# First attention: q/k projection half a step earlier with more buffers, blank writes moved to the dense stage, x in pieces, constants reordered

## The chip, the cores and the metric

One core of a Trainium2 chip runs the whole kernel. The metric is the device time of one execution in microseconds (us).

## What is computed

The kernel is four layers, each with a residual sum and a layer norm. The change is in the first, an attention block over 64-token buckets; the dense layers behind it take over one job of it. The first attention, cut:

```python
h = _ln(x, ln1_g, ln1_b)                      # x: 16 x 256 tokens x 128 channels
q, k, v = split(h @ w_qkv + b_qkv, 3)         # 16 heads of 8 channels, buckets of 64
kc = concatenate([kp, kb]); vc = concatenate([vp, vb])   # previous bucket and own
scores = einsum('bnihd,bnjhd->bnhij', qb, kc) * scale    # causal in the own bucket
attn = softmax(where(mask, scores, -inf))
x = x + einsum('bnhij,bnjhd->bnihd', attn, vc) @ w_out + b_out
# then an MLP, a gated dense layer of 8 experts, a second attention and a routed layer
```

## The kernel before

The first attention (`attention_0`) works through 16 batches (`NB`) of 256 tokens, software pipelined. The table `PARTS_0` is the order, written out by hand: four parts a step, each a list of (what, stage, k). `parts_0` runs 21 steps; in step s an entry works on batch s - stage. Every engine walks the same table and executes, in order, what it has under that name, so an engine's queue is its own extract of the table, and semaphores tie the queues together. Under the names stand:

- `stats` (VectorE: mean and variance of x, L445 to L449), `power` (GpSimd: inverse deviation, four small instructions, L319 to L322), `norm` (ScalarE: hn, L371), `lift` (TensorE transposes hn into the left half of the PSUM tile WA, L516, ScalarE copies it to hT; from batch 4 on, the same entry also transposes the attention output of four batches back into the right half, L520, copied to aT).
- `qk` (TensorE: q and k projections into WA, L526 and L527; ScalarE: copy with bias, L385, then the high part in f16, L389; GpSimd: the low part, L338). `spread` (SyncE): high and low part are written to a buffer in memory (`spill`, L282, L284), and six DMAs read them back (L298) into the row layout of the tiles qs (2 buffers) and ks (3 buffers).
- `scores` (TensorE: two units of eight matmuls, L548, and one mask matmul, L554; VectorE: row maxima, L463), four times a step; `mpad` and `shift` (VectorE, TensorE L560, VectorE L480: the maxima are subtracted from q, into q2); `weights` (TensorE: transposed scores in ST, L570; ScalarE: exponential into pt, L395; GpSimd: causal mask, L351; two units each); `values` (TensorE: pt times va into OT, L582); `copy`, `back` (L591), `output` (L601) to the result x1; `sums` (GpSimd: x1 + x, L344).
- `vproj` (TensorE L533, VectorE L457): value projection into va (3 buffers).

S and ST each have two halves, one per unit, so TensorE runs at most two units ahead of the maxima or of the exponentials. The tile MI is shared by `shift` and `back`, WB by `vproj` and `output`.

SyncE issues the DMAs of the loop: the spread of a batch; behind batch 0 the rest of x (tiles 12 to 31) and the gate; behind batch 1 the dense stage's first weights (`fetch_dense`); and from batch 1 on five blank writes a batch (L307, 268 KB each, 72 in all), which fill a table in memory for the last layer.

VectorE and GpSimd set the constants at the start: the k buffers are cleared and get a column added (L420), the v buffers get zeros and a column of ones, and the output bias is split into bf16 rows (`constants_of`). All of it stands in front of step 1.

In the dense stage, SyncE loads one broadcast gate row per job (L796) into a ring of six, paced by the semaphore `g_used`.

Of the kernel before, what the change touches and what calls it, by code (L numbers as in the profile page):

```python
# [9 lines left out]
P = 128  # L10
# [125 lines left out]
def unpacked(m, name):  # L136
# [4 lines left out]
    for part, shape in parts:  # L141
# [11 lines left out]
    [("qk", 1, 0), ("scores", 2, 0), ("shift", 3, 1), ("stats", 0, 0), ("weights", 3, 0), ("values", 4, 3),  # L153
     ("copy", 4, 1), ("spread", 1, 0)],
    [("scores", 2, 1), ("mpad", 2, 0), ("output", 5, 0), ("back", 4, 1), ("power", 0, 0), ("weights", 3, 1),
     ("values", 3, 0)],
    [("scores", 2, 2), ("vproj", 1, 0), ("shift", 2, 0), ("norm", 0, 0), ("weights", 3, 2), ("sums", 5, 0),
     ("values", 3, 1), ("copy", 3, 0)],
    [("lift", 0, 0), ("scores", 2, 3), ("mpad", 2, 1), ("back", 3, 0), ("weights", 3, 3), ("values", 3, 2)]]
STAGES_0 = 6  # L160


def parts_0(step):

    for s in range(NB + STAGES_0 - 1):
        for part in PARTS_0:
            for what, stage, k in part:
                if what == "lift":
                    if s < NB + 4:
                        step(what, s, k)  # L170
                elif 0 <= s - stage < NB:
                    step(what, s - stage, k)


def attention_0(nc, d, keep, rows, spill, stages):
# [3 lines left out]
    with ExitStack() as ctx:  # L179
# [10 lines left out]
        blank = m.sb("blank", [P, 4, ROW])  # L190
        blanks = rows.rearrange("(i p r) c -> p i r c", p=P, r=4)
        blank_set, blanked = m.sem("blank_set"), m.sem("blanked")
# [12 lines left out]
        qs = [m.sb(f"qs{p}", [P, 4, TB], F16) for p in range(2)]  # L205
        ks = [m.sb(f"ks{p}", [P, 4, BK + TB], F16) for p in range(3)]
        va = [m.sb(f"va{p}", [P, 4, H, 32]) for p in range(3)]
# [27 lines left out]
        lift_full, lift_free = m.sem("lift_full"), m.sem("lift_free")  # L235
        qk_full, qk_own, low_done = m.sem("qk_full"), m.sem("qk_own"), m.sem("low_done")
# [18 lines left out]
        LOADS, CLEARS, PRESET = 3, 5, 3  # L255
        READS = 16 * len(SPREAD)
        first_in, half_set, warm = m.sem("first_in"), m.sem("half_set"), m.sem("warm")
        preset, bias_own, bias_set = m.sem("preset"), m.sem("bias_own"), m.sem("bias_set")
        scrap = m.sb("scrap", [P, 2])

        def rows_landed(eng, n):
            eng.wait_ge(x_first if n < 2 else x_mid if n < 6 else x_rest, 16)
# [6 lines left out]
        def _(sp):  # L269
# [8 lines left out]
            def step(what, n, k):  # L278
                if what == "spread":
# [5 lines left out]
                    if n == 0:  # L285
                        sp.wait_ge(preset, PRESET)

                    wait(sp, mt_free, n * 2 - 2)
                    wait(sp, st_full, n * 8 - 16)
                    sp.wait_ge(spilled_high, 16 * (n + 1))  # L290
                    for part in range(2):
                        if part == 1:
                            sp.wait_ge(spilled_low, 16 * (n + 1))
                        for w, r, of in SPREAD:
                            if of == part:
                                dst = ks[n % 3][r::4, :, BK:BK + TB] if w else qs[n % 2][r::4, :, :]
                                src = spill[n % 2, of, w].rearrange("(a i) t -> i a t", a=4)
                                sp.dma_start(dst, src).then_inc(spread_done[n % 2], 16)  # L298
                    if n == 0:
                        sp.dma_start(x[:, 12:NT, :], d["x"][:, 12:NT, :]).then_inc(x_rest, 16)  # L300
                        sp.dma_start(keep["gate0"][:], d["gate0"]).then_inc(gate_in, 16)
                    if n == 1:
                        keep["fetch_dense"](sp)
                        sp.wait_ge(blank_set, 1)
                    if n:
                        for i in range(5 * n - 5, min(5 * n, BLANKS * NC_)):
                            sp.dma_start(blanks[:, i], blank[:]).then_inc(blanked, 16)  # L307

            parts_0(step)
            sp.wait_ge(blanked, 16 * BLANKS * NC_)  # L310

        @block.gpsimd
        def _(pool):
# [15 lines left out]
            pool.memset(va[2][:], 0.0).then_inc(zeroed, 1)  # L329
            pool.wait_ge(zeroed, 3)  # L330
            pool.memset(va[2][:, :, :, HD:HD + 1], 1.0).then_inc(cleared, 1)
            pool.memset(blank[:], BLANK).then_inc(blank_set, 1)

            def step(what, n, k):
                if what == "qk":
# [22 lines left out]
        def _(act):  # L358
# [6 lines left out]
            def step(what, n, k):  # L365
# [8 lines left out]
                if what == "lift":  # L374
                    act.wait_ge(lift_full, n + 1)
                    if n < NB:
                        ins = act.activation(hT[:, BK:BK + TB], WA[:, 0:TB], ACT.Identity, scale=g1, bias=s1)
                    if n >= 4:
                        ins = act.activation(aT[:], WA[:, TB:2 * TB], ACT.Copy)
                    ins.then_inc(lift_free, 1)  # L380
# [24 lines left out]
        def _(dve):  # L405
# [4 lines left out]
            for v in ks:  # L410
                dve.memset(v[:], 0.0).then_inc(bias_own, 1)

            def constants_of():
                dve.wait_ge(zeroed, 2)
                for v in va[0:2]:
                    dve.memset(v[:, :, :, HD:HD + 1], 1.0).then_inc(cleared, 1)
                dve.wait_ge(first_in, 32)
                dve.wait_ge(bias_own, 3)
                for i, v in enumerate(ks):
                    ins = dve.tensor_scalar(v[:].rearrange("p a t -> p (a t)"), v[:].rearrange("p a t -> p (a t)"),  # L420
                                            cols[:, 5:6], None, ALU.add)
                ins.then_inc(preset, 1)
# [3 lines left out]
                dve.wait_ge(bias_own, 4)  # L426
                t = Tally(dve, bias_own, 0, 0)
                t.n = 4
# [9 lines left out]
            def step(what, n, k):  # L438
                if what == "stats":
# [10 lines left out]
                    if n == 0:  # L450
                        constants_of()
                if what == "vproj":
                    dve.wait_ge(vproj_full, n + 1)
                    if n == 0:
                        dve.wait_ge(zeroed, 3)
                    wait(dve, pv_done, n * 8 - 16)
                    dve.tensor_tensor(va[n % 3][:, :, :, 0:HD],  # L457
# [18 lines left out]
                if what == "shift":  # L476
# [3 lines left out]
                    dve.tensor_tensor(q2[:, k], qs[n % 2][:, :, k * P:(k + 1) * P], MT,  # L480
# [20 lines left out]
        def _(pe):  # L501
# [7 lines left out]
            def step(what, n, k):  # L509
                if what == "lift":  # L510
                    wait(pe, lift_free, n)
                    wait(pe, high_done, min(n, NB))
                    if n < NB:
                        pe.wait_ge(hn_done, n + 1)
                        for a in range(2):
                            ins = pe.transpose(WA[:, a * P:(a + 1) * P], hn[:, a, :], ident[:])  # L516
                    if n >= 4:
                        pe.wait_ge(back_free, n * 2 - 6)
                        for a in range(2):
                            ins = pe.transpose(WA[:, TB + a * P:TB + (a + 1) * P], ob[n % 2][:, a, :], ident[:])  # L520
                    ins.then_inc(lift_full, 1)
                if what == "qk":
                    pe.wait_ge(lift_free, n + 1)
                    if n == 0:
# [4 lines left out]
                if what == "vproj":  # L529
                    wait(pe, x1_done, n - 3)  # L530
# [5 lines left out]
                if what == "scores":  # L536
# [5 lines left out]
                    for u in (2 * k, 2 * k + 1):  # L542
                        wait(pe, s_free, n * 8 + u - 1)
                        r = slice(32 * (u % 4), 32 * (u % 4) + 32)
                        for v in range(2):
                            w = 2 * (u // 4) + v
                            for a in range(4):
                                pe.matmul(S[BK * v:BK * v + BK, u % 2, a * P:(a + 1) * P],  # L548
                                          qs[n % 2][r, a, w * BK:(w + 1) * BK],
                                          ks[n % 3][r, a, w * BK:w * BK + P],  # L550
# [11 lines left out]
                if what == "weights":  # L562
                    t = k // 2
                    pe.wait_ge(mt_free, n * 2 + t + 1)
                    for u in (2 * k, 2 * k + 1):
                        wait(pe, exp_done, n * 8 + u - 1)
                        r = slice(32 * (u % 4), 32 * (u % 4) + 32)
                        for v in range(2):
                            for a in range(4):
                                ins = pe.matmul(ST[:, u % 2, (4 * v + a) * BK:(4 * v + a + 1) * BK],  # L570
                                                ks[n % 3][r, a, (2 * t + v) * BK:(2 * t + v) * BK + P],
                                                q2[r, t, a, v * BK:(v + 1) * BK], start=True, stop=True)
                        ins.then_inc(st_full, 1)
                if what == "values":
                    t = k // 2
                    wait(pe, ot_free, n * 2 + t)
                    pe.wait_ge(va_done, n + 1)
                    for u in (2 * k, 2 * k + 1):
                        pe.wait_ge(causal_done, n * 8 + u + 1)
                        for v in range(2):  # L580
                            for a in range(4):
                                ins = pe.matmul(OT[32 * a:32 * a + 32, (u % 4) * P + v * BK:(u % 4) * P + (v + 1) * BK],  # L582
                                                va[n % 3][:, 2 * t + v, 4 * a + u % 4, :],
# [1829 lines left out]
```

## Time and profile before

| | us |
|---|---|
| median of three runs (1057.59 to 1060.05) | 1059.03 |
| the profiled execution | 1057.45 |
| its span, first to last instruction | 1055.7 |
| busy TensorE / VectorE / ScalarE / GpSimd | 920.4 / 822.1 / 743.7 / 429.4 |
| mean granted TensorE clock, 1 being 2.4 GHz | 0.944 |

Busy is the time in which an engine executes instructions; the rest is idle, and the trace names what ended it. The first attention ends on TensorE at 238.7 us; the dense layers follow to about 680 us. In the timeline, a row is a group of like instructions in a row: start, length in us, engine, line, operation, output and inputs, count, and in brackets the idle time before and what ended it. SPq is SyncE's queue; its rows are the issuing of DMAs.

### The profile page before, as it was taken

What the parts mean: (1) busy time and instruction counts of PE and PEld (TensorE: products, weight loads), DVE (VectorE), ACT (ScalarE), POOL (GpSimd) and SP (SyncE); (2) the same over time, 40 slices, a digit from 0 to 9 for tenths busy, and PEclk for the clock granted to TensorE, in tenths of its full rate; (3) what the DMA queues carried; (4) which work ended last, traced back from release to release, by engine and by line L of the source; (5) the groups of instructions that cost most, each with busy time, mean ns of one, the idle gap of its engine ahead of it and who ended that gap; (6) DMA issues with size and microseconds to landing.
All of it is one profiled execution on the core that took longest, in us unless ns stands there. A gap on an engine that the chain in (4) does not pass through costs nothing. (4 is left out here: it accounts for less than half of the span.)

```text
span 1055.7 us, 28520 instructions
## 1 busy us (share of the span) xinstructions
PE 920.4 (87%) x9982; PEld 586.6 (56%) x9982; DVE 822.1 (78%) x2266; ACT 743.7 (70%) x1460; POOL 429.4 (41%) x600
## 2 busy tenths in 40 slices
PE   4899999984888999999999999678888875899995
PEld 2677777762444444444444444246556643788862
DVE  5567777746888999868899999858888866888854
ACT  2466666645889988888888878347677643688854
POOL 4356666653355000000000000023578877667653
PEclk8689999997999999999999999979999985999998
DMA  4545554500001200032222222011011102232218
GB/s 143 180 137 178 169 166 160 166 28 21 1 21 60 72 1 1 5 101 74 77 70 78 83 67 74 20 54 31 24 51 53 55 27 74 76 85 84 84 49 219
DMA packets 81946, 82.34 MB, mean 78 GB/s; under 512 B 9466, under 2 KB 58876, under 8 KB 81808
## 3 DMA queue, kind: packets, MB, share of 16 engines
q1 hardware_dynamic: 72608, 69.33, 21.5%
q0 software_dynamic: 4544, 8.60, 2.5%
q10 hardware_dynamic: 4656, 2.59, 1.0%
q8 instruction: 84, 1.38, 0.5%
q14 instruction: 54, 0.44, 0.1%
HBM read 45.71 MB, written 35.68 MB: 77 GB/s over the span
## 5 line engine op out<-in xcount | busy, mean ns | idle before, releaser
L840 ACT ACTIVATE d__hf<-d__HB,dense__d 128x512 f32<-128x512 f32 x288 | 184.7, 679 | 39.1 <-PE d__HB L1079 38.1
L899 DVE TENSOR_TENSOR d__hl<-d__hf,d__hh 128x1024 f16<-128x1024 f32 x144 | 173.5, 1219 | 19.9 <-ACT d__hh L845 17.8
L813 POOL TENSOR_SCALAR d__rstd<-d__mv 128x4 f32<-128x4 f32 x16 | 13.9, 868 | 353.1 <-DVE d__mv L1022 353.1
L845 ACT ACTIVATE d__hh<-d__hf 128x1024 f16<-128x1024 f32 x144 | 152.2, 1057 | 4.6
L463 DVE TENSOR_REDUCE a__mx<-a__S 128x4 f32<-128x512 f32 x128 | 82.1, 684 | 64.1 <-PE a__S L554 64.0
L395 ACT ACTIVATE a__pt<-a__ST 128x512 f32<-128x512 f32 x128 | 69.4, 594 | 63.7 <-PE a__ST L570 63.5
L1077 PE MATMUL d__YB<-d__hh,d__w2h 128*128 128x512 f16 x288 | 109.7, 381 | 2.5 <-DVE d__tmp L956 2.5
L1077 PE MATMUL d__HB<-d__xh,d__w1h 128*128 128x512 f16 x288 | 110.6, 384 | 0.0
L1078 PE MATMUL d__HB<-d__xl,d__w1h 128*128 128x512 f16 x288 | 110.5, 384 | 0.0
L1079 PE MATMUL d__HB<-d__xh,d__w1l 128*128 128x512 f16 x288 | 110.3, 383 | 0.0
L1078 PE MATMUL d__YB<-d__hl,d__w2h 128*128 128x512 f16 x288 | 109.7, 381 | 0.0
L1079 PE MATMUL d__YB<-d__hh,d__w2l 128*128 128x512 f16 x288 | 109.4, 380 | 0.0
L351 POOL TENSOR_SCALAR_AFFINE_SELECT a__pt<-a__pt 128x512 f32<-128x512 f32 x128 | 81.3, 659 | 56.5 <-ACT a__pt L395 56.3
L1338 POOL DMA_INDIRECT parts<-c__ys,c__dest x78 | 81.0, 1038 | 39.1 <-issue 16.8
L1824 POOL DMA_INDIRECT rows<-b__xr,b__slot x64 | 63.8, 996 | 21.5 <-issue 17.0
L1356 ACT ACTIVATE c__hf<-b__SS,c__bias 128x256 f32<-128x256 f32 x156 | 61.0, 474 | 7.3 <-PE b__SS L1565 6.2
L1492 DVE TENSOR_TENSOR c__hl<-c__hf,c__hh 128x512 f16<-128x512 f32 x78 | 54.3, 696 | 2.7
L1077 PEld LDWEIGHTS d__YB<-d__hh,d__w2h 128*128 128x128 f16 x288 | 28.3, 98 | 35.9 <-DVE d__tmp L956 3.9
L1079 PEld LDWEIGHTS d__HB<-d__xh,d__w1l 128*128 128x128 f16 x288 | 28.4, 99 | 35.0 <-issue 1.7
L1077 PEld LDWEIGHTS d__HB<-d__xh,d__w1h 128*128 128x128 f16 x288 | 30.4, 106 | 31.1 <-issue 1.4
L1079 PEld LDWEIGHTS d__YB<-d__hh,d__w2l 128*128 128x128 f16 x288 | 28.3, 98 | 34.3 <-issue 0.6
L582 PE MATMUL a__OT<-a__pt,a__va 128*32 128x64 f32 x2048 | 44.8, 229 | 1.6 <-POOL a__pt L351 0.9
(405 smaller groups left out, 2418.8 us busy)
## 6 DMA issues: line engine op xcount, KB each, us to landing
rows<-a__blank SPq DMA_DIRECT2D x72, 268.0 KB, 3.4
d__G<-gates SPq DMA_DIRECT2D x64, 256.0 KB, 3.2
c__xin<-rows SPq DMA_DIRECT2D x39, 134.0 KB, 2.3
dense__stage<-e_w SPq DMA_DIRECT2D x16, 256.0 KB, 2.9
b__stage<-e_w SPq DMA_DIRECT2D x32, 128.0 KB, 2.2
a__qs<-spill SPq DMA_DIRECT2D x48, 64.0 KB, 2.3
a__ks<-spill SPq DMA_DIRECT2D x48, 64.0 KB, 2.5
spill<-a__high SPq DMA_DIRECT2D x16, 128.0 KB, 4.0
```

Of the source, the lines that this page charges most:

```text
L351: pool.affine_select(out=v, in_=v, compare_op=ALU.is_ge, fill=0.0, base=BK, pattern=[[0, 8], [1, BK]], channel_multiplier=-1).then_inc(cau ...
L395: act.activation(pt[:, u % 4, :], ST[:, u % 2, :], ACT.Exp, scale=scale).then_inc(exp_done, 1)
L463: dve.tensor_reduce(mx[:, u // 4, :, u % 4], S[:, u % 2, :].rearrange("p (a j) -> p a j", a=4), AX.X, ALU.max).then_inc(s_free, 1)
L840: act.activation(hf[:, q, f], HB[:, f], gelu, scale=1.0 / WS, bias=b1[:, at:at + 1]).then_inc(s_["h_free"], 1)
L845: act.activation(hh[:, j % (LEAD + 1), f - 1:f + 1], hf[:, q, f - 1:f + 1], ACT.Copy).then_inc(s_["hi_done"], 1)
L899: dve.tensor_tensor(hl[:, p, f], hf[:, q, f], hh[:, p, f], ALU.subtract).then_inc(s_["lo%d_done" % i], 1)
L1077: pe.matmul(dst, wh, vh, start=begin, stop=False)
L1078: pe.matmul(dst, wh, vl, start=False, stop=False)
L1079: return pe.matmul(dst, wl, vh, start=False, stop=end)
L1338: pool.indirect_dma_start(parts, bass.IndirectOffsetOnAxis(dest[b % RING][:, a:a + 1], 0), ys[b % RING][:, a, :], None, bounds_check=2 * T ...
L1356: ins = act.activation(hf[b % 2][:, f], HB[:, b % 2, f // 2, f % 2], ACT.Gelu, scale=1.0 / WS, bias=bias[:, f, b:b + 1])
L1824: pool.indirect_dma_start(rows, bass.IndirectOffsetOnAxis(slot[n % SENT][:, k, a:a + 1], 0), words[n % SENT][:, a, :], None, bounds_check= ...
```

## The change

- `PARTS_0` has seven stages (22 steps). `norm` and `lift` of a batch come in the step after its `stats`, `qk` in part 2 of that step, `scores` at stage 3. GpSimd's part of `qk` is an entry of its own, `low`; the output's transpose is one too, `turn`, at stage 5.
- q tiles have 3 buffers, k and v tiles 4. The waits for old readers match.
- The 72 blank writes are issued in the dense stage, one behind each gate load, a second one behind each of the first eight. The tile and its semaphore move to `keep`, and a memset on GpSimd fills it, as before.
- Tiles 12 to 31 of x come in five pieces, behind the spreads of batches 0 to 4. The gate comes behind batch 2, the dense weights behind batch 6.
- The k buffers are set by one copy each, behind the statistics of batches 0 to 3, the bias rows behind those of batch 4; GpSimd sets the ones of all v buffers.

```diff
@@ -150,14 +150,14 @@
...
-    [("qk", 1, 0), ("scores", 2, 0), ("shift", 3, 1), ("stats", 0, 0), ("weights", 3, 0), ("values", 4, 3),
-     ("copy", 4, 1), ("spread", 1, 0)],
-    [("scores", 2, 1), ("mpad", 2, 0), ("output", 5, 0), ("back", 4, 1), ("power", 0, 0), ("weights", 3, 1),
-     ("values", 3, 0)],
-    [("scores", 2, 2), ("vproj", 1, 0), ("shift", 2, 0), ("norm", 0, 0), ("weights", 3, 2), ("sums", 5, 0),
-     ("values", 3, 1), ("copy", 3, 0)],
-    [("lift", 0, 0), ("scores", 2, 3), ("mpad", 2, 1), ("back", 3, 0), ("weights", 3, 3), ("values", 3, 2)]]
-STAGES_0 = 6
+    [("norm", 1, 0), ("scores", 3, 0), ("shift", 4, 1), ("weights", 4, 0), ("values", 5, 3), ("copy", 5, 1)],
+    [("scores", 3, 1), ("mpad", 3, 0), ("lift", 1, 0), ("output", 6, 0), ("back", 5, 1), ("weights", 4, 1),
+     ("values", 4, 0)],
+    [("qk", 1, 0), ("scores", 3, 2), ("shift", 3, 0), ("stats", 0, 0), ("weights", 4, 2), ("low", 1, 0),
+     ("spread", 1, 0), ("sums", 6, 0), ("values", 4, 1), ("copy", 4, 0)],
+    [("scores", 3, 3), ("mpad", 3, 1), ("vproj", 1, 0), ("power", 0, 0), ("back", 4, 0), ("weights", 4, 3),
+     ("values", 4, 2), ("turn", 5, 0)]]
+STAGES_0 = 7
...
 def parts_0(step):
@@ -165,10 +165,7 @@
...
-                if what == "lift":
-                    if s < NB + 4:
-                        step(what, s, k)
-                elif 0 <= s - stage < NB:
+                if 0 <= s - stage < NB:
@@ -202,9 +196,9 @@
...
-        qs = [m.sb(f"qs{p}", [P, 4, TB], F16) for p in range(2)]
-        ks = [m.sb(f"ks{p}", [P, 4, BK + TB], F16) for p in range(3)]
-        va = [m.sb(f"va{p}", [P, 4, H, 32]) for p in range(3)]
+        qs = [m.sb(f"qs{p}", [P, 4, TB], F16) for p in range(3)]
+        ks = [m.sb(f"ks{p}", [P, 4, BK + TB], F16) for p in range(4)]
+        va = [m.sb(f"va{p}", [P, 4, H, 32]) for p in range(4)]
@@ -252,14 +247,18 @@
...
-        LOADS, CLEARS, PRESET = 3, 5, 3
+        LOADS, CLEARS, PRESET = 3, 2, 3
...
+        ones_set = m.sem("ones_set")
...
         def rows_landed(eng, n):
-            eng.wait_ge(x_first if n < 2 else x_mid if n < 6 else x_rest, 16)
+            if n < 6:
+                eng.wait_ge(x_first if n < 2 else x_mid, 16)
+            else:
+                eng.wait_ge(x_rest, 16 * ((n - 6) // 2 + 1))
@@ -282,32 +281,29 @@
...
-                    if n == 0:
-                        sp.wait_ge(preset, PRESET)
-                    wait(sp, mt_free, n * 2 - 2)
-                    wait(sp, st_full, n * 8 - 16)
+                    if n < 4:
+                        sp.wait_ge(preset, PRESET + n + 1)
+                    wait(sp, mt_free, n * 2 - 4)
+                    wait(sp, st_full, n * 8 - 24)
...
-                                dst = ks[n % 3][r::4, :, BK:BK + TB] if w else qs[n % 2][r::4, :, :]
+                                dst = ks[n % 4][r::4, :, BK:BK + TB] if w else qs[n % 3][r::4, :, :]
...
-                    if n == 0:
-                        sp.dma_start(x[:, 12:NT, :], d["x"][:, 12:NT, :]).then_inc(x_rest, 16)
+                    if 12 + 4 * n < NT:
+                        cut = slice(12 + 4 * n, 16 + 4 * n)
+                        sp.dma_start(x[:, cut, :], d["x"][:, cut, :]).then_inc(x_rest, 16)
+                    if n == 2:
...
-                    if n == 1:
+                    if n == 6:
...
-                        sp.wait_ge(blank_set, 1)
-                    if n:
-                        for i in range(5 * n - 5, min(5 * n, BLANKS * NC_)):
-                            sp.dma_start(blanks[:, i], blank[:]).then_inc(blanked, 16)
...
-            sp.wait_ge(blanked, 16 * BLANKS * NC_)
...
         @block.gpsimd
         def _(pool):
@@ -326,13 +322,15 @@
...
-            pool.memset(va[2][:], 0.0).then_inc(zeroed, 1)
-            pool.wait_ge(zeroed, 3)
-            pool.memset(va[2][:, :, :, HD:HD + 1], 1.0).then_inc(cleared, 1)
-            pool.memset(blank[:], BLANK).then_inc(blank_set, 1)
+            for v in va[2:4]:
+                pool.memset(v[:], 0.0).then_inc(zeroed, 1)
+            pool.wait_ge(zeroed, 4)
+            for v in va:
+                pool.memset(v[:, :, :, HD:HD + 1], 1.0).then_inc(ones_set, 1)
+            pool.memset(keep["blank"][:], BLANK).then_inc(keep["blank_set"], 1)
...
             def step(what, n, k):
-                if what == "qk":
+                if what == "low":
@@ -373,11 +371,11 @@
...
                 if what == "lift":
...
-                    if n < NB:
-                        ins = act.activation(hT[:, BK:BK + TB], WA[:, 0:TB], ACT.Identity, scale=g1, bias=s1)
-                    if n >= 4:
-                        ins = act.activation(aT[:], WA[:, TB:2 * TB], ACT.Copy)
-                    ins.then_inc(lift_free, 1)
+                    act.activation(hT[:, BK:BK + TB], WA[:, 0:TB], ACT.Identity, scale=g1,
+                                   bias=s1).then_inc(lift_free, 1)
+                if what == "turn":
+                    act.wait_ge(turn_full, n + 1)
+                    act.activation(aT[:], WA[:, TB:2 * TB], ACT.Copy).then_inc(turn_free, 1)
                 if what == "qk":
@@ -407,25 +405,19 @@
...
-            for v in ks:
-                dve.memset(v[:], 0.0).then_inc(bias_own, 1)
-            def constants_of():
-                dve.wait_ge(zeroed, 2)
-                for v in va[0:2]:
-                    dve.memset(v[:, :, :, HD:HD + 1], 1.0).then_inc(cleared, 1)
+            def key_rows(i):
...
-                dve.wait_ge(bias_own, 3)
-                for i, v in enumerate(ks):
-                    ins = dve.tensor_scalar(v[:].rearrange("p a t -> p (a t)"), v[:].rearrange("p a t -> p (a t)"),
-                                            cols[:, 5:6], None, ALU.add)
-                ins.then_inc(preset, 1)
+                v = ks[i][:].rearrange("p a t -> p (a t)")
+                dve.tensor_copy(v, cols[:, 5:6].to_broadcast([P, 4 * (BK + TB)])).then_inc(preset, 1)
+            def bias_rows():
...
-                dve.wait_ge(bias_own, 4)
+                dve.wait_ge(bias_own, 1)
...
-                t.n = 4
+                t.n = 1
@@ -447,14 +439,18 @@
...
-                    if n == 0:
-                        constants_of()
+                    if n < 4:
+                        key_rows(n)
+                    if n == 4:
+                        bias_rows()
                 if what == "vproj":
...
-                        dve.wait_ge(zeroed, 3)
-                    wait(dve, pv_done, n * 8 - 16)
-                    dve.tensor_tensor(va[n % 3][:, :, :, 0:HD],
+                        dve.wait_ge(loaded, 16 * LOADS)
+                    if n < 4:
+                        dve.wait_ge(zeroed, 4 if n > 1 else 2)
+                    wait(dve, pv_done, n * 8 - 24)
+                    dve.tensor_tensor(va[n % 4][:, :, :, 0:HD],
...
                 if what == "scores":
@@ -509,25 +505,28 @@
             def step(what, n, k):
                 if what == "lift":
...
-                    wait(pe, high_done, min(n, NB))
-                    if n < NB:
-                        pe.wait_ge(hn_done, n + 1)
-                        for a in range(2):
-                            ins = pe.transpose(WA[:, a * P:(a + 1) * P], hn[:, a, :], ident[:])
-                    if n >= 4:
-                        pe.wait_ge(back_free, n * 2 - 6)
-                        for a in range(2):
-                            ins = pe.transpose(WA[:, TB + a * P:TB + (a + 1) * P], ob[n % 2][:, a, :], ident[:])
+                    wait(pe, qk_own, 2 * n)
+                    pe.wait_ge(hn_done, n + 1)
+                    for a in range(2):
+                        ins = pe.transpose(WA[:, a * P:(a + 1) * P], hn[:, a, :], ident[:])
...
+                if what == "turn":
+                    wait(pe, turn_free, n)
+                    pe.wait_ge(qk_own, 2 * min(n + 5, NB))
+                    pe.wait_ge(back_free, n * 2 + 2)
+                    for a in range(2):
+                        ins = pe.transpose(WA[:, TB + a * P:TB + (a + 1) * P], ob[n % 2][:, a, :], ident[:])
+                    ins.then_inc(turn_full, 1)
                 if what == "qk":
...
+                    wait(pe, turn_free, n - 4)
...
                 if what == "vproj":
-                    wait(pe, x1_done, n - 3)
+                    wait(pe, x1_done, n - 4)
@@ -568,19 +567,21 @@
...
-                                                ks[n % 3][r, a, (2 * t + v) * BK:(2 * t + v) * BK + P],
+                                                ks[n % 4][r, a, (2 * t + v) * BK:(2 * t + v) * BK + P],
...
                 if what == "values":
...
+                    if n == 0 and k == 0:
+                        pe.wait_ge(ones_set, 4)
...
-                                                va[n % 3][:, 2 * t + v, 4 * a + u % 4, :],
+                                                va[n % 4][:, 2 * t + v, 4 * a + u % 4, :],
@@ -594,8 +595,8 @@
...
-                    pe.wait_ge(lift_free, n + 5)
-                    pe.wait_ge(va_done, min(n + 4, NB))
+                    pe.wait_ge(turn_free, n + 1)
+                    pe.wait_ge(va_done, min(n + 5, NB))
@@ -795,6 +799,10 @@
...
+                for i in (k, k + len(order)):
+                    if i < BLANKS * NC_:
+                        sp.dma_start(blanks[:, i], keep["blank"][:]).then_inc(s_["blanked"], 16)
+            sp.wait_ge(s_["blanked"], 16 * BLANKS * NC_)
...
         @block.gpsimd
         def _(pool):
```

## Rows read from the trace of the kernel before

**Rows 1.** Windows: stretch, length, busy us (x instructions) per engine, clock, DMA share, GB/s.
```profile
33.50:43.70 10.20, 9.74 (x170) 7.73 (x174) 6.25 (x15) 3.61 (x8) 4.59 (x9) 0.50 0.79 264
50.60:60.80 10.20, 10.20 (x173) 8.13 (x165) 6.15 (x16) 3.53 (x7) 3.87 (x8) 0.50 0.52 169
65.60:201.60 136.00, 127.58 (x3315) 103.31 (x3315) 97.90 (x264) 91.38 (x187) 90.16 (x155) 1.00 0.50 160
214.40:217.80 3.40, 3.40 (x60) 2.93 (x58) 2.24 (x5) 1.65 (x3) 1.27 (x2) 0.50 0.02 5
```

**Rows 2.** Waits, 0 to 240 us: us in total, times, longest us.
```profile
PE a__S L548 <- DMA a__ks<-spill: 14.2, 13, 2.7
```

**Rows 3.** Timeline, PE, start us, us, line, op, tiles, count: starts of steps.
```profile
33.96 0.68 PE L548 MATMUL a__S<-a__ks,a__qs 32*64 32x128 f16 x16 [2.48 <-DMA a__ks<-spill]
...
50.41 0.60 PE L548 MATMUL a__S<-a__ks,a__qs 32*64 32x128 f16 x16 [2.68 <-DMA a__ks<-spill]
...
213.00 0.45 PE L548 MATMUL a__S<-a__ks,a__qs 32*64 32x128 f16 x16 [1.06 <-DMA a__ks<-spill]
```

**Rows 4.** Timeline, SPq: start us and us of the issuing.
```profile
164.03 3.68 SPq L307 DMA_DIRECT2D rows<-a__blank  x5
...
167.80 0.48 SPq L282 DMA_DIRECT2D spill<-a__high  x1
```

**Rows 5.** Timeline, PE, a step in which no wait shows.
```profile
165.82 0.45 PE L548 MATMUL a__S<-a__ks,a__qs 32*64 32x128 f16 x16 [1.16 <-DMA a__ks<-spill]
...
166.75 0.54 PE L570 MATMUL a__ST<-a__q,a__ks 32*128 32x64 f16 x16
...
167.22 0.65 PE L582 MATMUL a__OT<-a__pt,a__va 128*32 128x64 f32 x32
...
167.80 0.49 PE L548 MATMUL a__S<-a__ks,a__qs 32*64 32x128 f16 x16
...
170.59 0.45 PE L548 MATMUL a__S<-a__ks,a__qs 32*64 32x128 f16 x16
...
173.46 0.44 PE L516 MATMUL a__WA<-keep__ident,a__hn 128*128 128x128 f32 x2
...
173.73 0.38 PE L520 MATMUL a__WA<-keep__ident,a__ob 128*128 128x128 f32 x2
...
176.24 0.70 PE L526 MATMUL a__WA<-a__hT,a__a 128*128 128x256 f32 x2
...
177.30 0.45 PE L548 MATMUL a__S<-a__ks,a__qs 32*64 32x128 f16 x16
```

**Rows 6.** Timeline, ACT, in and behind that step.
```profile
165.57 0.63 ACT L389 ACTIVATE a__high<-a__qk 128x512 f16<-128x512 f32 x1
...
167.19 1.08 ACT L395 ACTIVATE a__pt<-a__ST 128x512 f32<-128x512 f32 x2 [0.99 <-PE a__ST L570]
...
177.41 0.84 ACT L385 ACTIVATE a__qk<-a__WA,a__a 128x256 f32<-128x256 f32 x2 [0.70 <-PE a__WA L527]
```

**Rows 7.** Timeline, POOL, in that step.
```profile
167.95 1.27 POOL L351 TENSOR_SCALAR_AFFINE_SELECT a__pt<-a__pt 128x512 f32<-128x512 f32 x2 [0.52 <-ACT a__pt L395]
...
169.31 0.22 POOL L319 TENSOR_SCALAR a__mean_off<-a__mv 128x2 f32<-128x2 f32 x1
...
170.80 1.28 POOL L351 TENSOR_SCALAR_AFFINE_SELECT a__pt<-a__pt 128x512 f32<-128x512 f32 x2
...
174.84 0.72 POOL L344 TENSOR_TENSOR dense__xs<-dense__x,a__x 128x256 f32<-128x256 f32 x1
```

**Rows 8.** Tile a__low: count, duration ns min/median/max, first and last start.
```profile
L338 POOL TENSOR_TENSOR a__low<-a__qk,a__high x16: 1152/1156/1167, 13.7 to 203.2; 128x512 f16<-128x512 f32 x16
```

**Rows 9.** Groups of instructions, 0 to 240 us: DVE's constants (busy us, mean ns).
```profile
L420 DVE TENSOR_SCALAR a__ks<-a__ks,a__a 128x1280 f16<-128x1280 f16 x3 | 3.2, 1107 | 0.8 <-DMA a__a<-a 0.8
```

**Rows 10.** Windows, columns as in rows 1: the bias rows on DVE.
```profile
9.60:12.30 2.70, 2.29 (x7) 1.94 (x7) 2.36 (x12) 0.54 (x2) 0.65 (x2) 1.00 0.00 0
```

**Rows 11.** Timeline, PE: the value projection at the low clock.
```profile
26.94 1.91 PE L533 MATMUL a__WB<-a__a,a__hT 128*128 128x128 f32 x8
```

More of the change, by code:

```diff
@@ L189, in attention_0 @@
         onesb = m.sb("onesb", [P, P], BF16)
-        blank = m.sb("blank", [P, 4, ROW])
-        blanks = rows.rearrange("(i p r) c -> p i r c", p=P, r=4)
-        blank_set, blanked = m.sem("blank_set"), m.sem("blanked")
         x = m.sb("x", [P, NT, C])
@@ L235, in attention_0 @@
         lift_full, lift_free = m.sem("lift_full"), m.sem("lift_free")
+        turn_full, turn_free = m.sem("turn_full"), m.sem("turn_free")
         qk_full, qk_own, low_done = m.sem("qk_full"), m.sem("qk_own"), m.sem("low_done")
@@ L479, in step @@
                     wait(dve, st_full, n * 8 - 4 + 4 * k)
-                    dve.tensor_tensor(q2[:, k], qs[n % 2][:, :, k * P:(k + 1) * P], MT,
+                    dve.tensor_tensor(q2[:, k], qs[n % 3][:, :, k * P:(k + 1) * P], MT,
                                       ALU.subtract).then_inc(mt_free, 1)
@@ L548, in step @@
                                 pe.matmul(S[BK * v:BK * v + BK, u % 2, a * P:(a + 1) * P],
-                                          qs[n % 2][r, a, w * BK:(w + 1) * BK],
-                                          ks[n % 3][r, a, w * BK:w * BK + P],
+                                          qs[n % 3][r, a, w * BK:(w + 1) * BK],
+                                          ks[n % 4][r, a, w * BK:w * BK + P],
                                           start=(a == 0), stop=False, skip_group_check=True)
@@ L743, in dense_0 @@
                  "pb_full pb_free qb_full qb_free xh0_done xT_done xh1_done xl1_done var_done rstd_done xn_done "
-                 "own counted raw_done gt_done sent g_used acc_done fold_own b2_done")
+                 "own counted raw_done gt_done sent g_used acc_done fold_own b2_done blanked")
         s_ = {n: m.sem(n) for n in names.split()}
@@ L779, in dense_0 @@
         block = ctx.enter_context(nc.Block())
+        blanks = rows.rearrange("(i p r) c -> p i r c", p=P, r=4)
         @block.sync
         def _(sp):
+            sp.wait_ge(keep["blank_set"], 1)
             for j in range(2, E + 1):
@@ L2238, in program @@
         keep = {"ident": m.sb("ident", [P, P]), "gate0": m.sb("gate0", [P, E]),
-                "xa": m.sb("xa", [P, NT, C]), "logits": m.sb("logits", [P, NT, E])}
+                "xa": m.sb("xa", [P, NT, C]), "logits": m.sb("logits", [P, NT, E]),
+                "blank": m.sb("blank", [P, 4, ROW]), "blank_set": m.sem("blank_set")}
         tiles = {}
```

## The prediction, made before the kernel was run

> **What bounds the kernel now.** I read the windows first, for where TensorE is full and at which clock, then the waits of the first attention, then the timeline of a few steps. The change touches the first 240 us; the rest is read only for what is moved into it. In the pipelined middle of this attention, eleven steps in 136.0 us, the matmul engine is busy 127.58 us at full clock, VectorE 97.90, ScalarE 91.38 and GpSimd 90.16 [rows 1]: TensorE bounds it, and what it waits for is time. The wait with a name is that of the score matmuls for the q and k rows that come back from memory: 14.2 us in 13 places [rows 2]. Two large ones lie in the filling (2.48 and 2.68 us), one at the end (1.06) [rows 3].
>
> A step in which no such wait falls runs from 165.82 to 177.30 us, 11.48 us [rows 5]. Eleven of these are 126.3 us, so the middle holds 9.7 us above it, 0.9 a step. The cause is on the DMA queue: in one step SyncE issues five blank writes from 164.03 for 3.68 us, while ScalarE has the high parts ready at 165.57 + 0.63 = 166.20; their spill is issued at 167.80, 1.6 us late [rows 4, 6].
>
> **The clock.** Three stretches behind the waits of rows 3 are at the lower level (0.50, which is 1.2 GHz): two of 10.2 us and one of 3.4 us. At 2.4 GHz the middle issues 3315 matmuls in 127.58 busy us, 26.0 a us; 173 of them are then worth 6.7 us, so a 10.2 us stretch costs 3.5 us, and the short one with 60 matmuls costs 1.1 us [rows 1, 3].
>
> **Part by part, the middle.** The new table moves the q/k projection from the head of part 0 to the head of part 2, the transpose before it to part 1, and has the scores read them at stage 3 and not 2. From projection to scores there is now a step and a half; the third q buffer and the fourth k and v buffers let the spread start without waiting for old readers; the blank writes are gone from the queue in front of it. Each alone would take most of the 9.7 us, so all 9.7 us are taken off. The new and split waits on TensorE (the lift on the copies of the last projection, the turn on this one's, the first values on the ones) are for things finished at least a part earlier and cost nothing.
>
> What is late next is GpSimd's queue. Before, its orders are: part 0 low part and one pair of masks (W0), part 1 power and W1, part 2 W2 and the sums, part 3 W3. After: part 0 W0, part 1 W1, part 2 W2, low part, sums, part 3 power, W3. Five jobs now stand in one row, and behind them TensorE's last values matmuls (V3), which have also moved nearer, because the projection no longer stands in front of them in part 0. With T the start of the q/k projection on TensorE, in part 2:
> - ScalarE starts its copy at T + 1.17 (176.24 to 177.41), for 0.84, then the high part for 0.63, so the exponentials of W2 start at T + 2.68 [rows 5, 6]; GpSimd follows 0.76 later (167.19 to 167.95), at T + 3.44 [rows 6, 7].
> - W2 1.27, low part 1.16, sums 0.72, power 1.49 (169.31 to 170.80), W3 1.28: 5.92, so W3 is ready at T + 9.36 [rows 7, 8].
> - V3 takes 0.58 (167.22 to 167.80), its second half 0.29 [rows 5]: it ends at T + 9.65.
> - Then part 1: the old one is 2.79 (167.80 to 170.59), the lift adds 0.27 (173.46 to 173.73) [rows 5], and the next projection starts at T + 12.71.
>
> So the loop through GpSimd is 12.7 us long where TensorE's own work is 11.48: a wait of 1.23 us a step in front of V3. It applies after the steps with all five jobs, ten of them, and once without sums (0.51): 12.8 us. **Middle: 12.8 - 9.7 = +3.1 us.** How sure is 1.23? From below it is nothing, if GpSimd's jobs overlap more than their rows say; from above some 1.6, if VectorE, which now has the values bias add in part 3, also holds up the shift in part 0. That second wait would lie inside the first, as both are on the same part. I take the sum as it stands, with 0.4 a step either way, 4 us.
>
> A rule that speaks against the moved row of jobs: GpSimd's low part lasted 1152 to 1167 ns in all sixteen steps, whatever VectorE did beside it [rows 8]. The Trainium skill (SBUF — State Buffer, Who interferes with whom) says that a VectorE instruction with two inputs in SBUF keeps out a GpSimd instruction that reads SBUF. If each step's subtraction of the maxima hit the row of jobs, the loop would be longer than above; the row shows no such lengthening beyond 15 ns, and nothing is added.
>
> **The filling.** Taken off: the waits of 2.48 and 2.68 us, since the piece of x is now 4 tiles, and the dense weights and the blanks are no longer between one spill and the next: -5.2. Put on: the second value projection now stands in front of the first scores, 1.7 us of new work at the low clock (1.91 with its tail) [rows 11]; the k buffer's constants, 1.1 us on VectorE [rows 9], now fall into its work for steps 0 to 3, where three lie in idle time and the fourth in front of a maximum that TensorE needs: +1.1; the bias rows, 2.36 busy of 2.70 us in the idle start before [rows 10], now stand in the statistics of step 4, in front of another maximum: +2.7; GpSimd's row without sums: +0.5. That is +0.8. The clock: both 10.2 us stretches follow waits that go, but the constants put a wait of 1 to 2 us in about the same place. I take one stretch as saved, -3.5, with none and two as bounds. **Filling: -2.7, from -6.2 to +0.8.** The added seventh stage is otherwise free: the same work with other step numbers.
>
> **The end.** The wait of 1.06 goes, and with it the 3.4 us at low clock (-1.1). One value projection fewer lies here, about 0.95 at full clock, half of rows 11. There are now two steps with neither projection; their parts are shorter than the chain from weights to values, +0.5 by estimate. **End: -2.6,** between -3.5 and 0.
>
> **Edits at nothing.** x in five pieces: the first is needed by step 6's statistics and issued after the first spread; if late, VectorE's statistics wait, then the whole head. Gate and dense weights at steps 2 and 6: needed 40 us later or more. The 72 blank writes in the dense stage: SyncE's issue of 0.74 each [rows 4] stands in front of the next gate load, and the loads run six jobs ahead; if that lead were gone, the accumulation on VectorE would wait for gates. Bounds 0 and +1. The clear of three more buffers at the start is hidden behind the x load.
>
> **The sum.** +3.1 - 2.7 - 2.6 = -2.2 against the profiled execution of 1057.45: 1055.25. The median of the three is 1.6 above that execution, so 1056.8.
>
> **Rivals.** (A) GpSimd's row doesn't bind: for it speaks that it is busy only 90.16 of 136.0 us [rows 1]; against it, that its order is fixed and the five jobs follow each other. Then the middle is -9.7, the filling 0.5 less, in all 2.2 + 12.8 + 0.5 = 15.5 us off: 1043.5. (B) Slower: the wait of 1.2 us before V3, in each of ten steps, puts TensorE on the low clock, as the wait of 1.06 did at the end [rows 1, 3]. Each 10.2 us stretch costs 3.5. One gives 1060.3, 1.3 above the median before; it decides from the second on (1063.8), and with three it is 1067.3. Against it: the middle before had waits such as the 1.16 us at 165.82, and its clock stayed at 1.00 throughout [rows 1, 5]. [...] (C) The spread is still late and the scores wait as before: only possible if the DMA queue is held by something else than the blanks. Then 12.8 of GpSimd's wait falls together with it: about 1060.
>
> **Chances.** Forecast 0.70 (by itself 1051 to 1063), A 0.13, B 0.13, C 0.04. 0.2% of this kernel is 2.1 us, about what a measurement can tell from no change. Faster by more than that (under 1056.9): all of A, half of the forecast's case, 0.48. Within: 0.25 of the forecast's and some of B and C, 0.28. Slower: 0.24. The range leaves out the lower half of A and the upper half of B: 1045 to 1067.
>
> **What would show it.** Right: the profile's scores have no DMA in front; V3 (the values matmuls behind the weights of part 0) waits for GpSimd's mask about 1.2 us a step, step length 12.7; GpSimd's row W2, low, sums, power, W3 without gaps; the first scores about 1.7 us later. Wrong: steps of 11.5 (A); low clock inside the middle (B); waits of the scores for the spill (C); gate waits in the dense stage.

## The result and the profile after

The changed kernel takes 1066.26 us in the median of 11 runs (1062.19 to 1068.33); the kernel before, on the same chips, 1058.53 (1056.02 to 1064.84). The ratio is 1.0065, 95% interval 1.0044 to 1.0086: slower by 0.65%, where 1056.8 us and rather a gain had been forecast. The profiled execution has a span of 1064.5 us, 8.8 more than before.

Where the 8.8 us lie, from the timelines of TensorE: the first attention ends at 244.02 us and not at 238.70 (+5.3); the dense stage behind it takes 449.5 us in both (0); all behind it takes 371.0 and not 367.6 (+3.4), in code that the change doesn't touch. The attention splits into filling -1.7 (the full steps start at 63.88 and not 65.62), middle +8.7 (eleven steps, from the scores of batch 3 to those of batch 14: 144.68 us, to 208.56, where it was 135.94, to 201.56), end -1.7.

GpSimd's queue in one step of the changed kernel, from the timeline (start, us, engine, line, operation; in brackets the idle time before):

```profile
72.64 1.27 POOL L349 TENSOR_SCALAR_AFFINE_SELECT a__pt<-a__pt 128x512 f32<-128x512 f32 x2 [1.90 <-ACT a__pt L393]
...
73.87 1.16 POOL L336 TENSOR_TENSOR a__low<-a__qk,a__high 128x512 f16<-128x512 f32 x1
...
74.99 0.74 POOL L342 TENSOR_TENSOR dense__xs<-dense__x,a__x 128x256 f32<-128x256 f32 x1
...
75.79 0.22 POOL L315 TENSOR_SCALAR a__mean_off<-a__mv 128x2 f32<-128x2 f32 x1
...
77.29 1.28 POOL L349 TENSOR_SCALAR_AFFINE_SELECT a__pt<-a__pt 128x512 f32<-128x512 f32 x2
```

These are W2, the low part, the sums, power (four instructions, of which the first stands here) and W3, without a gap: 72.64 to 78.57 is 5.93 us, forecast from rows 7 and 8 as 5.92. TensorE's rows of the same step:

```profile
76.23 0.39 PE L553 MATMUL a__S<-a__abf 128*128 128x256 bf16 x2
...
77.00 0.38 PE L559 MATMUL a__MI<-a__a,a__mpad 128*128 128x128 f16 x4 [0.38 <-DVE a__ob L485]
77.32 0.54 PE L569 MATMUL a__ST<-a__q,a__ks 32*128 32x64 f16 x16
...
78.10 0.95 PE L583 MATMUL a__OT<-a__pt,a__va 128*32 128x64 f32 x32 [0.24 <-POOL a__pt L349]
...
78.62 0.27 PEld L583 LDWEIGHTS a__OT<-a__pt,a__va 128*32 128x32 f32 x16 [0.25 <-POOL a__pt L349]
```

V3 (L583) waits for both halves of W3, and the shift before it (L559) waits for VectorE. Most of what the step lost stands in three places: 0.38 us idle before the shift, 0.24 idle before V3, and V3 itself, whose matmuls last from 78.10 to 79.05 where rows 5 have 0.65 for the same ones. No score matmul waits for the spill any more, against rows 2 and 3.

The windows of two steps of the changed kernel and of its whole middle (columns as in rows 1):

```profile
69.32:81.94 12.62, 11.91 (x307) 9.37 (x301) 9.52 (x24) 8.38 (x18) 8.18 (x14) 1.00 0.29 82
81.94:96.12 14.18, 13.45 (x308) 10.62 (x301) 9.96 (x25) 8.42 (x18) 8.19 (x14) 0.88 0.26 74
63.88:208.56 144.68, 137.13 (x3313) 108.15 (x3312) 105.04 (x261) 92.47 (x188) 89.58 (x153) 0.95 0.22 63
```

A step is 12.62 us at full clock; the next one, with the same work, has a clock of 0.88 and is 1.56 longer. The stretches at the lower level (1.2 GHz) are 3.4 us each, at 91.4, 118.8, 132.4 and 197.3; before there was none in this place (clock 1.00 in rows 1). Each begins 0.4 to 1.3 us behind the start of a V3 that had waited (the first of these V3 starts at 90.74).

### The profile page after: what moved, and what is told of

Its sections match the earlier page's. It is cut to its first block and busy times, and to the rows that moved or that the text cites. A ratio compares the mean times of both kernels' runs of the same rounds, so it can differ in the third digit from the quotient of the medians.

```text
span 1064.5 us, 28549 instructions
## 1 busy us (share of the span) xinstructions
PE 934.3 (88%) x9982; PEld 592.7 (56%) x9982; DVE 832.8 (78%) x2263; ACT 745.8 (70%) x1460; POOL 433.0 (41%) x604
## 5 line engine op out<-in xcount | busy, mean ns | idle before, releaser
L583 PE MATMUL a__OT<-a__pt,a__va 128*32 128x64 f32 x2048 | 46.8, 228 | 4.1 <-POOL a__pt L349 3.0
```

## The experiments

Runs on one chip are compared with the kernel before on that chip. A ratio is to that kernel's median, with the 95% interval. "Attention ends" is the last output matmul of the first attention in the one profile of each kernel; two profiles of the kernel before differ by 7 us in it (below), two of the changed kernel by 1.3.

**The row of jobs taken apart.** The changed kernel, with this edit of the table:

```diff
-    [... ("weights", 4, 0), ("values", 5, 3), ...
+    [... ("stats", 0, 0), ("weights", 4, 0), ("values", 5, 3), ...
-     ... ("back", 5, 1), ("weights", 4, 1), ...
+     ... ("back", 5, 1), ("power", 0, 0), ("weights", 4, 1), ...
-     ... ("stats", 0, 0), ("weights", 4, 2), ("low", 1, 0), ("spread", 1, 0), ("sums", 6, 0), ...
+     ... ("weights", 4, 2), ("low", 1, 0), ("spread", 1, 0), ...
-     ... ("power", 0, 0), ("back", 4, 0), ("weights", 4, 3), ...
+     ... ("back", 4, 0), ("weights", 4, 3), ("sums", 6, 0), ...
```

> The changed kernel with GpSimd's five jobs in a row taken apart: stats in part 0, power in part 1 ahead of W1 (as before the change), sums in part 3 behind W3; all else as changed. Theory (the row W2, low, sums, power, W3 is the loop): the step in the middle falls from 12.63 to about 11.5 us, V3 waits no more, the 3.4 us stretches at low clock in the middle go; the first attention ends some 17 us earlier than in the changed kernel, total about 1048 to 1050. Rival (the long step is TensorE's clock or another engine's chain): the step stays over 12.3 us.

Measured: 1047.27 us, just under the range expected, ratio 0.991 (0.988 to 0.9941) to the kernel before. Attention ends at 225.06, 19 us earlier than in the changed kernel. One wait for the spill, of 3.1 us, stands in the filling. The window of ten steps:

```profile
65.90:182.50 116.60, 116.49 (x3022) 93.45 (x3010) 94.32 (x238) 83.87 (x172) 81.03 (x137) 1.00 0.25 72
```

TensorE is busy 116.49 of 116.60 us, the clock is 1.00, a step lies between 11.55 and 12.05. Ten steps take 116.6 us where the changed kernel takes 132.7 (69.32 to 202.03), 16 of the 19 us. Taking the row apart, with each job as long as it was, gives back the wait and, in this profile, the clock. The edit also moves VectorE's statistics, on which `power` waits, so it is not GpSimd's order alone; the next two edits touch nothing else.

**One job out of the row.** Only `("sums", 6, 0)` is moved, behind W3.

> The changed kernel with one job of the row moved: sums behind W3. Theory: the loop shortens by the 0.72 us of that job, to a step of 11.9 us, and VectorE's subtraction of the maxima is no longer held up by it, so that the 0.38 us wait of the shift goes as well. With waits of half the size, the 3.4 us low-clock stretches in the middle (four before) are fewer. Total about 1055. Rival: the step moves by less than 0.3 us.

Measured: 1055.56 us, ratio 0.9999 (0.9972 to 1.0025); attention ends at 232.56. Eight of the steps are 11.93 to 11.95 us: 0.68 shorter for 0.72 of work. No low-clock stretch between 62 and 225 us. VectorE's subtraction for the maxima (L470) takes 0.26 us where it takes 0.68 beside the sums in the changed kernel; it starts here just after the low part has ended (112.23 + 1.16 = 113.39):

```profile
113.48 0.26 DVE L470 TENSOR_TENSOR a__mpad<-a__mx,a__mpad 128x16 f16<-128x16 f32 x1
```

```profile
75.13 0.68 DVE L470 TENSOR_TENSOR a__mpad<-a__mx,a__mpad 128x16 f16<-128x16 f32 x1
```

(the first is this kernel's timeline, the second the changed kernel's).

**A longer row.** The changed kernel with the sums twice; the second result goes to a spare tile that nobody reads.

```diff
                     pool.tensor_tensor(keep["xs"][:, cut, :], keep["x1"][:, cut, :], x[:, cut, :], ALU.add)
+                    pool.tensor_tensor(spare[:, cut, :], keep["x1"][:, cut, :], x[:, cut, :], ALU.add)
```

> The changed kernel with the row made longer: the sums job twice, its second result into a spare tile that nobody reads. Theory: the step goes from 12.63 to 13.36 us (0.73 for the job), ten times, 7 us; and with a wait of 1.9 us a step the stretches at low clock in the middle become more than the four of the changed kernel; total 1073 to 1080. Rival (the step is set elsewhere): under 3 us slower.

Measured: 1072.57 us, ratio 1.0102 (1.0055 to 1.0149), about 6 us more than the changed kernel's median on other chips and just under the range expected. The full-clock steps are 13.29 to 13.31 us, 0.68 more. So three lengths of the row, 0.7 us apart, give three lengths of the step, 0.68 apart. But the low clock in the middle did not become more, as had been expected: three stretches (of 3.4, 3.4 and 6.8 us) against four, 13.6 us in both, although V3 now waits 0.9 us in every step. The profile is the slowest of the five executions (1078.29 us).

**The blanks alone.** The kernel before with the 72 blank writes issued in the dense stage, as in the change.

```diff
-                    if n:
-                        for i in range(5 * n - 5, min(5 * n, BLANKS * NC_)):
-                            sp.dma_start(blanks[:, i], blank[:]).then_inc(blanked, 16)
+                for i in (k, k + len(order)):
+                    if i < BLANKS * NC_:
+                        sp.dma_start(blanks[:, i], keep["blank"][:]).then_inc(s_["blanked"], 16)
```

> The kernel before with one part of the change alone: the 72 blank writes issued in the dense stage. Theory (the blanks in SyncE's queue were what made the scores wait): the waits of the scores for the spill shrink from 14.2 us to a few, the step falls from 12.4 to about 11.6, total 1046 to 1050. Rival (the spread is late by its own chain and needs the half step ahead): waits stay over 8 us, total over 1054.

Measured: 1042.2 us, ratio 0.9879 (0.9824 to 0.9934). Attention ends at 221.14. The wait of rows 2 is now

```profile
PE a__S L540 <- DMA a__ks<-spill: 3.2, 4, 2.3
```

with most of it (2.3) in the filling; most steps are 11.47 or 11.48 us. The high part's spill lands in 2.6 us in the median from 60 to 200 us, against 4.2 before. This one edit beats both kernels, and the total is 4 us below the range expected.

**The blanks back.** The changed kernel with the blank writes behind the spreads again.

> The changed kernel with the blank writes back behind the spreads. Theory: the step is set by GpSimd's row, and a step and a half is ample for the spread: the scores don't wait for the spill, the step stays at 12.63, total within 2 us of the changed kernel. Rival (the gain of the change lay in the blanks): waits for the spill come back and it is over 5 us slower.

Measured: 1063.31 us, ratio 1.0086 (1.0053 to 1.0118); no matmul waits for the spill, and the full-clock step is 12.61 to 12.63. So the half step ahead and the buffers do hide the blanks; with them hidden, moving them gains nothing more. The profile has three stretches at low clock in the middle (of 6.8, 3.4 and 3.4 us), and the first two follow stops of TensorE of 1.36 and 1.14 us for which it names no cause:

```profile
76.36 0.41 PE L591 MATMUL a__OT<-a__pt,a__va 128*32 128x64 f32 x10 [1.36 <-issue]
...
105.64 0.44 PE L555 MATMUL a__S<-a__ks,a__qs 32*64 32x128 f16 x12 [1.14 <-issue]
```

**The other loads.** The blanks-only kernel with x in five pieces, the gate behind batch 2 and the dense weights behind batch 6.

> The blanks-only kernel with the other loads moved as in the change (x in five pieces, gate behind batch 2, dense weights behind batch 6), order table, buffers and constants as before the change. Theory (the one wait of 2.3 us that the blanks-only kernel keeps in the filling, and the 10.2 us at low clock there, come from the loads of x and the dense weights between the spills): wait and low-clock stretch go, first attention ends 3 to 6 us earlier, total 1036 to 1040. Rival (the wait is the spread's own latency behind the projection): it stays at 2 us or more, total 1041 to 1043.

Measured: 1043.72 us, ratio 0.9847 (0.98 to 0.9893). The wait of 2.3 us in the filling is gone; the full steps' first projection stands at 64.77 and not at 69.11. But attention ends only 1.1 us earlier, at 220.02, and the total misses the 1036 to 1040 expected and is no better clear of noise (the intervals of the two ratios overlap): one step in the middle takes 15.39 us. In it TensorE stands still from 94.35 with nothing named as its cause, 4 us behind the issuing of the dense weights at 87.86 to 90.36, and then has 3.4 us at low clock:

```profile
96.22 0.44 PE L579 MATMUL a__OT<-a__pt,a__va 128*32 128x64 f32 x6 [1.87 <-issue]
```

The trace has one hint. The DMA queue that the profile calls instruction (q8) moves 16 KB every 4.8 us on average from 50 to 222 us; while the weights are in transfer it moves nothing from 86.8 to 93.9 us, and the stop begins 0.4 us later. The three unnamed stops of 1.36, 1.14 and 0.58 us in the kernel with the blanks back also follow the three longest such intervals of its middle (7.5, 8.4 and 7.1 us). But intervals of 7.0 to 7.5 us in other profiles (two in the changed kernel's) have no stop of that size behind them, and no run moved these transfers. That TensorE waits there for its instructions is an argument, not shown.

**The constants.** The changed kernel with `key_rows` for all four buffers and `bias_rows` behind the statistics of batch 0.

> The changed kernel with its constants set behind the statistics of batch 0, as before the change. Theory (the bias rows on VectorE in step 4 hold up the maxima): the wait of 2.70 us before the scores of step 5 and the 0.89 us behind it go, the first attention ends 3 to 7 us earlier, the middle stays at 12.63 a step; total 1058 to 1062. Rival: the filling is bound by the latency of the first steps and doesn't change by more than 1 us.

Measured: 1060.16 us, ratio 1.0013 (0.9987 to 1.0039). Of the two waits behind the bias rows the first is gone and the second is down to 0.32 us; these are they in the changed kernel's timeline:

```profile
48.75 0.92 PE L547 MATMUL a__S<-a__ks,a__qs 32*64 32x128 f16 x16 [2.70 <-DVE a__mx L459]
...
50.90 0.59 PE L559 MATMUL a__MI<-a__a,a__mpad 128*128 128x128 f16 x4 [0.89 <-DVE a__ob L485]
```

Attention ends at 236.44, 7.6 us earlier: the full steps' first projection stands 3.0 us earlier (66.27 for 69.32), ten steps take 127.2 us and not 132.7 (-5.5), the end is 1.0 longer. Most of the 5.5 are the clock: this profile has no low-clock stretch in the middle at all (but one of 23.9 us from 227.5, past the end), although most steps are 12.61 to 12.63 us as in the changed kernel and have the same waits. Since the changed kernel's own two profiles differ in these stretches, they are not shown to be gone because of the constants.

**Both repairs.** The split row and the early constants together.

> The changed kernel with both repairs: the row of jobs split (stats in part 0, power in part 1, sums behind W3) and the constants behind the statistics of batch 0. Theory (row and constants are all that the change lost): step 11.5 us as in the kernels without the row, no wait of over 1 us before the scores in the filling, first attention ends 3 to 5 us before that of the split row alone (225.06), near 221, total 1041 to 1045, level with the blanks-only kernel, because once the blanks are gone the half step ahead has nothing left to hide. Rival (the half step ahead still gains by itself): under 1040.

Measured: 1046.84 us, ratio 0.9881 (0.9845 to 0.9916); attention ends at 223.67, 1.4 us before the split row alone, less than the 3 to 5 expected: one wait of 1.6 us for the spill stands in the filling. The total is 2 us above the range expected and not below 1040: with the blanks gone, no gain of the half step ahead by itself shows.

**Second profiles.** The changed kernel and the kernel before, once more each.

> The changed kernel once more, for a second profile. The order of the work is the same, so the step of 12.63 us and the waits before V3 come back at the same places. If the low-clock stretches in the middle follow from where the waits happen to lie, their number and places may differ from the first profile (four of 3.4 us); if they follow from the work alone, they are the same. The part behind the dense stage, 3.4 us longer in the first profile than before the change, has unchanged code: expected within 368 to 373 us.

> The kernel before, for a second profile of its clock. Expected: waits of the scores for the spill of 12 to 16 us in all, no or few low-clock stretches between 65 and 202 us (none in the first profile), the part behind the dense stage between 366 and 372 us (367.6 in the first). If that part comes out at 371 here, the 3.4 us that it was longer in the changed kernel's profile are not the change's.

Changed, again: 1065.07 us, attention ends at 242.74, steps of 12.61 to 12.63 where the clock is full, low clock in the middle at 119.9 and 133.6 only, part behind the dense stage 371.0. Before, again: 1056.01 us, but attention ends at 231.48 and not at 238.70, since the scores' waits for the spill come to 7.4 us and not 14.2; the part behind the dense stage is 372.4, not 367.6. Ten steps of the kernel before, in the second profile and in the first:

```profile
75.60:193.90 118.30, 116.15 (x3020) 94.00 (x3010) 89.31 (x241) 83.33 (x172) 81.78 (x140) 1.00 0.53 172
```

```profile
76.00:200.40 124.40, 115.98 (x3018) 93.95 (x3010) 89.01 (x241) 83.09 (x172) 81.88 (x140) 1.00 0.52 167
```

TensorE's busy time is the same within 0.2 us; the waits differ by 6.

## Why the prediction was wrong, point by point

- **What bounds the middle, and what is late next: right.** GpSimd's row of five jobs replaced the blanks' wait: a step of 12.62 where 12.7 was worked out, 5.93 us of row where 5.92. (The start of the exponentials at T + 2.68 adds up to 2.64 from its own terms; it was 2.57, and nothing hangs on it.) Taking one job out, doubling it and splitting the row moved the step as the row's length says. What was off is the place: the 1.2 us were to show as one wait before V3, and only 0.24 stand there; the second wait, before the shift, and V3's own length hold most of the rest.
- **The middle's +3.1 us: this term failed.** Measured +8.7 in the same pair of profiles. The waits came nearly as priced (12.62 - 11.48 = 1.14 us a step for 1.23, so without the clock the middle would be about +2.5), but the clock was taken as staying at 1.00, and what rival B described happened in a smaller form: stretches of 3.4 us, not 10.2, each worth 14.18 - 12.62 = 1.56 us, four in the first profile (6.2 us). B had been argued away by the waits in the kernel before, which reached 1.16 us [rows 5] and left the clock full [rows 1]. The runs show that this argument doesn't carry: of the kernels with the row, two profiles of the changed one have four and two such stretches, the longer row and the blanks back three each, the early constants none; of seven profiles without the long row (before twice, blanks only, with the other loads, split row, both repairs, one job out) only the one with the unnamed stop of 1.87 us has one. All twelve in the kernels with the row, but the first two of the blanks back, begin within 1.5 us of the start of a V3 that had waited. So the stretches go with the row's waits or with unnamed stops, and not in every execution; yet single waits of 1.54 and 1.59 us in the two profiles of the kernel before, longer than any before V3, brought none. Why a given wait brings one is open. B had a chance of 0.13, and the time came out where it puts two to three long stretches (1063.8 to 1067.3). The wait of 1.54 us:

```profile
90.75 0.45 PE L548 MATMUL a__S<-a__ks,a__qs 32*64 32x128 f16 x16 [1.54 <-DMA a__ks<-spill]
```

- **The basis: one profile of the kernel before.** The -9.7 in this term was read from one execution whose waits for the spill were 14.2 us; another has 7.4, and from its ten steps (118.3 us) instead of the first's (124.4) the change had about 6 us less to take away. And its part behind the dense stage, 367.6, is the shortest seen; the other eleven profiles have 369.7 to 374.4. So the +3.4 us there are not the change's. Between the two profiles of the kernel before, the attention differs by 7.2 us one way and this part by 4.9 the other, and the totals hide it. A sum made from one profile has to carry this.
- **The filling, -2.7: measured -1.7.** The bias rows cost more than they were priced at (2.70 + 0.89 us of wait for 2.7), which is most of the difference; a k buffer's copy takes 0.8 us and not 1.1. Low clock there: 6.8, 10.2 and 6.8 us, where 13.7 and twice 10.2 had been, in sum 10.3 us less; one stretch of 10.2 had been counted as saved.
- **The end, -2.6: measured -1.7.** A 3.4 us stretch at 238.2 replaced the one at 214.4, whose 1.1 us had been counted as saved.
- **The edits at nothing: right for the blanks.** In the dense stage the transfers doubled and TensorE's busy time in 200 us stayed (197.08 before, rows of the same window before and after):

```profile
450.00:650.00 200.00, 197.08 (x924) 90.47 (x923) 173.57 (x251) 171.98 (x225) 10.18 (x11) 1.00 0.26 80
```

```profile
450.00:650.00 200.00, 197.07 (x923) 90.36 (x921) 172.00 (x243) 172.32 (x225) 9.87 (x10) 1.00 0.52 168
```

- **The port rule.** The prediction added nothing for it, since GpSimd's low part never lengthened [rows 8]. GpSimd's row did not lengthen here either, but VectorE did: its subtraction takes 0.68 us and not 0.23 while the sums run on GpSimd (75.13 to 75.81, the sums end at 75.73), and the shift waits 0.38 us for what stands behind it. The prediction had asked only whether GpSimd would be kept out. The Trainium skill (SBUF — State Buffer, Who interferes with whom) says that the order of issue decides which of the two is blocked; the trace agrees: the sums start at 74.99, the subtraction at 75.13, and VectorE is the one that waits. It seems to have cost nothing extra, since the shift's wait ends before W3 does; with the sums doubled the shift's wait stayed 0.38 and V3's grew by 0.7. No run took this away and left the row as long.

## What to carry to other kernels

When a hand-written order is changed, write out each engine's own extract of it and add up what now stands in a row in front of the next hand-over: here five jobs of unchanged length, moved next to each other, cost 1.14 us a step, more than the 0.9 that the change removed. Move one thing at a time where the trace names the cause: moving the blank writes alone gave 1.2%, and with them gone the pipeline rebuilt around them had nothing left to hide. And read a second profile of the kernel before when the sum is smaller than its waits vary.

## What the runs showed that was not expected

- Low-clock stretches in a stage whose matmul engine is busy 94% (11.91 of 12.62 us): none, two and four of 3.4 us in three profiles with the same step, 12.6 us at full clock.
- The same kernel with the same order has 7.4 or 14.2 us of waits for its spill, with 0.53 and 0.52 of the DMA engines busy.
- A GpSimd addition of 0.74 us holds a VectorE instruction of 0.23 us until its end, three times its length. The cast before it (L469) takes 0.40 us while the low part runs and 0.20 without.
